# Recurrence products and negated maxima in PSUM, the heads' root on VectorE, y and bonus summed ahead of centring

## The reference, cut to what matters

```
# layer 1, for each sequence, head (8 x 8 state s) and token
a     = k[:, None] * v[None, :]
out   = einsum(r, faaaa * a + s)        # r . s ("y") plus r . (faaaa * a) ("bonus")
s_new = a + w[:, None] * s
y = (y - mean8(y)) * rsqrt(var8(y) + 1e-5) * gn_w + gn_b   # per head of 8 channels
# layer 2, self and cross attention
scores = scores * mask - 10000 * (1 - mask)
probs  = softmax(scores)                # exp(scores - max) / sum
# layer norms: (x - mean) / sqrt(var + 1e-5)
```

## Time and profile before

| | |
|---|---|
| median of 3 runs | 1115.88 us (1115.58 to 1124.76) |
| the profiled execution, its own time | 1123.09 us |
| its span | 1121.3 us |
| TensorE busy | 1006.8 us (90%) |
| VectorE busy | 817.9 us (73%) |
| GpSimd busy | 567.8 us (51%) |
| ScalarE busy | 555.1 us (50%) |
| mean granted TensorE clock | 0.957 |

### The profile page before, as it was taken

The page is one execution under the profiler, slowest core; times in us unless marked ns, Lnnn a source line. Parts: engine busy times, 40 slices in busy tenths (PEclk is TensorE's granted clock), DMA queues, the critical chain, the costliest instruction groups (busy, mean ns, idle before and its releaser), DMA issues.

```text
span 1121.3 us, 27159 instructions
## 1 busy us (share of the span) xinstructions
PE 1006.8 (90%) x10816; PEld 802.3 (72%) x10816; DVE 817.9 (73%) x1679; ACT 555.1 (50%) x1354; POOL 567.8 (51%) x634
## 2 busy tenths in 40 slices
PE   5868999998777889999999999999987978999997
PEld 3647877766556678888877877776665757878886
DVE  1233268879999888988546357569998999997675
ACT  2479573322223236546676875642222333756663
POOL 1354155557565565554344354456655655664331
PEclk9979999989979899999999999999996988999999
DMA  8501000000000000000101010010000000000001
GB/s 345 212 2 25 25 25 1 25 0 1 1 1 1 2 31 1 32 32 2 52 22 45 10 38 23 3 25 1 1 1 1 1 2 12 2 13 12 12 2 40
DMA packets 28172, 30.35 MB, mean 27 GB/s; under 512 B 16528, under 2 KB 24976, under 8 KB 27280
## 3 DMA queue, kind: packets, MB, share of 16 engines
q1 hardware_dynamic: 28048, 28.63, 7.7%
HBM read 26.52 MB, written 2.10 MB: 26 GB/s over the span
## 4 chain that ended last, share of the span: by engine, by line
PE 56%; DVE 21%; DVEq 10%; issue 5%; POOL 3%; ACT 2%; POOLq 2%; ACTq 1%; DMA 1%; SPq 0%
PE bank L489 7%; PE bank L501 7%; PE bank L363 6%; PE bank L375 6%; PE bank L396 6%; PE bank L388 4%; DVEq L1006 3%; DVEq L864 3%; PE bank L520 3%; DVE lane L1010 3%; DVE lane L865 2%; PE bank L452 2%; PE bank L529 2%; DVE lane L809 2%; PE bank L432 2%
## 5 line engine op out<-in xcount | busy, mean ns | idle before, releaser
L1365 POOL TENSOR_TENSOR lane<-lane 128x512 f32<-128x512 f32 x160 | 166.6, 1047 | 220.8 <-DVE lane L884 126.2
L1164 ACT COPY lane<-bank 128x512 f32<-128x512 f32 x240 | 135.9, 587 | 216.7 <-PE bank L363 82.6
L363 PE MATMUL bank<-ident,lane 128*128 128x128 f32 x896 | 135.1, 287 | 26.0 <-DVE lane L809 15.4
L363 PEld LDWEIGHTS bank<-ident,lane 128*128 128x128 f32 x896 | 106.6, 146 | 53.2 <-DVE lane L809 18.5
L1433 POOL TENSOR_TENSOR lane<-lane 128x512 f32<-128x512 f32 x64 | 83.6, 1311 | 87.1 <-DVE lane L1010 87.1
L1010 DVE TENSOR_TENSOR_SCAN lane<-lane 128x256 f32<-128x256 f32 x128 | 99.9, 821 | 5.8
L1228 ACT ACTIVATE lane<-bank,lane 128x128 f32<-128x128 f32 x256 | 91.0, 374 | 25.9 <-DVE lane L934 24.7
L1186 ACT ACTIVATE lane<-lane 128x512 f32<-128x512 f32 x96 | 60.6, 635 | 72.9 <-DVE lane L865 72.5
L1146 ACT ACTIVATE lane<-bank,vecs 128x256 f32<-128x256 f32 x112 | 55.8, 552 | 73.1 <-PE bank L363 72.6
L1351 POOL TENSOR_TENSOR lane<-lane,scalars 128x2 f32<-128x2 f32 x56 | 41.2, 736 | 73.5 <-DVE lane L801 70.6
L882 DVE TENSOR_REDUCE lane<-lane 128x8 f32<-128x512 f32 x96 | 64.7, 674 | 11.6 <-ACT lane L1186 11.3
(11 more groups left out here) (157 smaller groups left out, 2293.1 us busy)
## 6 DMA issues: line engine op xcount, KB each, us to landing
lane<-in_inT SPq DMA_DIRECT2D x16, 256.0 KB, 5.2
lane<-in_x SPq DMA_DIRECT2D x16, 256.0 KB, 2.8
w_d<-in_w_d SPq DMA_DIRECT2D x1, 3072.0 KB, 24.6
w_am<-in_w_am SPq DMA_DIRECT2D x1, 2048.0 KB, 11.3
lane<-in_inT SPq DMA_DIRECT2D x16, 128.0 KB, 3.0
lane<-in_ctx SPq DMA_DIRECT2D x8, 256.0 KB, 2.7
out_x<-lane SPq DMA_DIRECT2D x8, 256.0 KB, 2.2
w_c<-in_w_c SPq DMA_DIRECT2D x1, 1792.0 KB, 15.6
```

The lines of the kernel that those rows point to most:

```text
L363: ins = pe.transpose(t[:, i * P:(i + 1) * P], src, ident[:, :])
L1164: s.copy(out, src).then_inc(bk.free_sem(key), 1)
L1365: p.tensor_tensor(q, q, den.unsqueeze(2).to_broadcast([P, n, 512 // n]), ALU.mult).then_inc(sig["normal"].sem, 1)
```

## The change

- `steps`: the copy of s0 by VectorE is gone. TensorE writes s0 into the token-0 columns of the spread bank by one more matmul per state pair, with the identity as weights and 8 columns moving; the spread matmuls write tokens 1 to 63. The tile of k is widened by one column per sequence, holding 1.0, so that VectorE multiplies all 512 elements of the bank by k in place in PSUM. The scans read the products from PSUM and write the state to SBUF. The bank is freed after the scans, by a drain of its own.
- `shift` and `masked`: in self and cross attention the negated maxima are written into the score bank (its first 8 columns, whose scores were already taken) and read from there by the addition that follows; the bank is freed by that addition, no longer by the masking. The signal "shifted" goes, and GpSimd waits for a new signal "masked". Layer 3 keeps its tile.
- y and bonus: VectorE adds the bonus to y on the way from the bank to SBUF, in place of ScalarE's copy; the centring is two matmuls a group (of 256 columns each) in place of four.
- The root: the seed, the Newton steps (three instructions each) and the spreading over sequences move from GpSimd to VectorE, behind the addition of 1e-5.
- `v_variance`: its drain and addition of 1e-5 move to GpSimd, ahead of the power, with a drain there. Statistics and application stay on VectorE.
- The mixes are opened as (w, k) and (v, r, g). TensorE waits for the small per-group input once before the first spread. All order strings and BANKS are new.

The diff, its core:

```
             def spread_values(m, i0):
                 t = [pe_open(pe, (g, "spread", m, i)) for i in (i0, i0 + 1)]
                 for e in range(2):
                     for n in range(2):
                         q = slice(32 * (i0 + n), 32 * (i0 + n) + 32)
-                        ins = pe.matmul(t[n][:, e * T:(e + 1) * T], spread[q, e, :], L.bv[q, m, :], start=True, stop=True)
-                        if e == 1:
-                            ins.then_inc(bk.full_sem((g, "spread", m, i0 + n)), 1)
+                        pe.matmul(tokens(t[n][:, e * T:(e + 1) * T])[:, :, 1:S], spread[q, e, :], tokens(L.bv[q, m, :])[:, :, 0:S - 1],
+                                  start=True, stop=True)
+                for n in range(2):
+                    i = i0 + n
+                    pe.matmul(t[n][:, :].rearrange("p (e b t) -> p e b t", e=2, b=G)[:, :, :, 0], ident[:, :], L.s0[:, m, 2 * i:2 * i + 2, :],
+                              start=True, stop=True).then_inc(bk.full_sem((g, "spread", m, i)), 1)
...
-                pe.matmul(t[:, m * T:(m + 1) * T], centre, L.bonus[:, m, :], start=True, stop=False)
-                ins = pe.matmul(t[:, m * T:(m + 1) * T], centre, L.yc[:, m, :], start=False, stop=True)
+                ins = pe.matmul(t[:, m * T:(m + 1) * T], centre, L.yc[:, m, :], start=True, stop=True)
...
             for tt in range(TT):
-                v.bn_aggr(L.mv[:, tt, :], L.stats[:, tt, :])
-            v.drain()
-            v.tensor_scalar(L.mv[:, :, 1], L.mv[:, :, 1], 1e-5, None, ALU.add).then_inc(sig["variance"].sem, 1)
+                ins = v.bn_aggr(L.mv[:, tt, :], L.stats[:, tt, :])
+            ins.then_inc(sig["variance"].sem, 1)
...
-            def shift(j, src):
-                v.tensor_reduce(A.nmax[:, j, :], src, AX_X, ALU.max, negate=True)
+            def shift(j, src, nmax):
+                v.tensor_reduce(nmax, src, AX_X, ALU.max, negate=True)
                 v.drain()
-                return v.tensor_tensor(grid(A.probs[j]), src, A.nmax[:, j, :].unsqueeze(2).to_broadcast([P, n, S]), ALU.add)
+                v.tensor_tensor(grid(A.probs[j]), src, nmax.unsqueeze(2).to_broadcast([P, n, S]),
+                                ALU.add).then_inc(bk.free_sem((g, tag, "scores", j)), 1)
...
-                    shift(j, grid(A.probs[j])).then_inc(sig["shifted"].sem, 1)
+                    shift(j, grid(A.probs[j]), bk.tile((g, tag, "scores", j))[:, 0:n])
...
                 st = L.state[:, 2 * i:2 * i + 2, :, :]
-                v.tensor_copy(st[:, :, :, 0], L.s0[:, m, 2 * i:2 * i + 2, :])
-                src = bk.tile(key)[:, :].rearrange("p (e b t) -> p e b t", e=2, b=G)
-                kt = tokens(L.bk[:, m, :])
-                v.tensor_tensor(st[:, :, :, 1:S], src[:, :, :, 0:S - 1],
-                                kt[:, :, 0:S - 1].unsqueeze(1).to_broadcast([P, 2, G, S - 1]), ALU.mult).then_inc(bk.free_sem(key), 1)
+                kv = bk.tile(key)[:, :].rearrange("p (e b t) -> p e b t", e=2, b=G)
+                v.tensor_tensor(kv, kv, L.bk[:, m, :, 0:S].unsqueeze(1).to_broadcast([P, 2, G, S]), ALU.mult)
                 v.drain()
                 w = L.wS[:, m, :, :].rearrange("p b t -> p (b t)")
                 for e in range(2):
-                    s = st[:, e, :, :].rearrange("p b t -> p (b t)")
-                    ins = v.tensor_tensor_scan(s, w, s, 0.0, ALU.mult, ALU.add)
+                    ins = v.tensor_tensor_scan(st[:, e, :, :].rearrange("p b t -> p (b t)"), w, bk.tile(key)[:, e * T:(e + 1) * T], 0.0,
+                                               ALU.mult, ALU.add)
                 ins.then_inc(sig["scanned"].sem, 1)
+                v.drain().then_inc(bk.free_sem(key), 1)
...
+            key = (g, "y")
+            v.wait_ge(bk.full_sem(key), bk.full_at(key))
+            v.tensor_tensor(flat(L.yc[:, :, :]), bk.tile(key)[:, :], flat(L.bonus), ALU.add).then_inc(bk.free_sem(key), 1)
+            yield
...
+            v.tensor_scalar(var, bk.tile(key)[:, 0:S], 1e-5, None, ALU.add).then_inc(bk.free_sem(key), 1)
+            v.drain()
+            v.tensor_scalar(r.bitcast(I32), var.bitcast(I32), -0.5, RSQRT_SEED, ALU.mult, ALU.add)
+            v.drain()
+            for _ in range(3):
+                v.tensor_tensor(t, r, r, ALU.mult)
+                v.drain()
+                v.scalar_tensor_tensor(t, t, -0.5, var, ALU.mult, ALU.mult)
+                v.drain()
+                v.scalar_tensor_tensor(r, t, 1.5, r, ALU.add, ALU.mult)
+                v.drain()
+            v.tensor_tensor(tokens(L.rstd_rows), r.unsqueeze(1).to_broadcast([P, G, S]), own_batch.unsqueeze(2).to_broadcast([P, G, S]),
+                            ALU.mult).then_inc(sig["rstd_own"].sem, 1)
...
+            else:
+                p.tensor_scalar(L.mv[:, :, 1], L.mv[:, :, 1], 1e-5, None, ALU.add)
+            p.drain()
```

More of the change, by code:

```diff
@@ L83 @@
     "PE": (
[L84 to L87, removed]
@@ L633, in pe_b @@
                 if n == 0:
-                    mix(MIXES[2:4])
+                    mix(MIXES[2:5])
                     yield
@@ L689, in pe_b @@
             yield
-            pe.wait_ge(bk.free_sem((g, "bonus")), bk.taken_at((g, "bonus")))
             pe.wait_ge(bk.free_sem((g, "y")), bk.taken_at((g, "y")))
@@ L895, in v_attention @@
                         v.wait_ge(bk.full_sem((g, tag, "scores", PT_ - 1)), bk.full_at((g, tag, "scores", PT_ - 1)))
-                    shift(j, grid(bk.tile(key)[:, :])).then_inc(bk.free_sem(key), 1)
+                    shift(j, grid(bk.tile(key)[:, :]), A.nmax[:, j, :])
                     yield
@@ L967, in v_b @@
             v.memset(L.wS[:, :, :, 0], 0.0)
+            v.memset(L.bk[:, :, :, 0], 1.0)
             yield
@@ L1372, in p_attention @@
                 if step < PT_ and tag != "l3":
-                    key = (g, tag, "scores", step)
-                    p.wait_ge(bk.free_sem(key), bk.taken_at(key))
+                    p.wait_ge(sig["masked"].sem, sig["masked"].at(g, PART[tag] + step + 1))
                     if tag == "self":
@@ L1434, in p_b @@
                     yield
-            key = (g, "var_y")
-            p.wait_ge(bk.free_sem(key), bk.taken_at(key))
-            x, r, t = L.yw[:, 0, :], L.yw[:, 1, :], L.yw[:, 2, :]
-            p.tensor_scalar(r.bitcast(I32), x.bitcast(I32), -0.5, RSQRT_SEED, ALU.mult, ALU.add)
-            p.drain()
-            for step in range(3):
-                p.tensor_tensor(t, r, r, ALU.mult)
-                p.drain()
-                p.tensor_tensor(t, t, x, ALU.mult)
-                p.drain()
-                p.tensor_scalar(t, t, -0.5, 1.5, ALU.mult, ALU.add)
-                p.drain()
-                p.tensor_tensor(r, t, r, ALU.mult)
-                p.drain()
-            p.tensor_tensor(tokens(L.rstd_rows), r.unsqueeze(1).to_broadcast([P, G, S]), own_batch.unsqueeze(2).to_broadcast([P, G, S]),
-                            ALU.mult).then_inc(sig["rstd_own"].sem, 1)
-            yield
         def p_c(p, g):
```

99 lines of the change are left out of this document (48 added, 51 removed).

## The result

The changed kernel takes **1088.66 us** (median of 4 runs, 1087.44 to 1090.60) against 1116.34 us (4 runs, 1115.58 to 1124.76) of the kernel before on the same chip: a ratio of **0.9737, 95% interval 0.9687 to 0.9787**. That is 27.7 us, more than double the 13 that I forecast, though inside the range; it is 4 us from the time that I gave to the rival "latency comes back too".

What follows compares the result with a forecast made beforehand. VectorE was taken to bound two stretches, TensorE the rest. VectorE's terms sum to -14 us, TensorE's to +1, so -13 from an expected median of 1115.9 gives 1103 us; range 1083 to 1127.

Steps and rivals of the forecast that it cites:

- latency comes back too: Faster rival: shorter root and relieved GpSimd leave TensorE fewer gaps in the VectorE stretches, clock stays up; 1085 us, chance 0.20.
- scans: VectorE's scans reading PSUM: 635 ns each, 68 of them in the VectorE stretches, -10.0 us.
- Identity matmuls: TensorE's 128 added records of 8 columns at 0.12 us each, +15 us, half in stretches that TensorE sets.
- the prediction's own rule: A microsecond off VectorE counts about one in the VectorE stretches, nearly nothing outside; the reverse holds for TensorE.
- the mixes: On TensorE, mix g runs beside two mixes using other rows of the array, saving 8 us.
- the root's term: Root moved to VectorE: 4.4 us a group, six groups in the VectorE stretches, +26 us; its shorter chain gives little.
- VectorE stretches: The windows 224 to 504 and 784 to 1008 us, where VectorE is busy 91% and TensorE idles 69.7 us.
- The 1e-5 of the layer norms: Addition and drain moved from VectorE to GpSimd, 32 of 48 in the VectorE stretches, taken as -11 us.
- the maxima: Negated maxima in PSUM: 60 two-SBUF additions in the VectorE stretches fall to 692 ns, -19.6 us.
- Paid back elsewhere: No-change rival: stretches shift, savings fall where TensorE is full, or GpSimd holds up the root; 1115 us, chance 0.22.
- Banks held too long: Slower rival: score banks freed 5.7 us later, TensorE waits at 16 openings; 1127 to 1135 us, chance 0.15, shared.
- Product in the same bank: Slower rival: reading and writing one PSUM bank takes turns, doubling the product instruction; 1126 us, within a shared 0.15.

Runs made afterwards that it cites:

- e11: The changed kernel without the identity matmuls, spreads again 256 columns wide, s0 left out: 1082.60 us, ratio 0.9676.
- e3: The changed kernel with the root back on GpSimd, all else kept: 1131.68 us, ratio 1.0120.
- e17: The kernel before with all parts of the change but the root, best searched orders: 1144.81 us (3 runs; a fourth took 1798.41), ratio 1.0209.
- e14: The work of the changed kernel under the best orders and banks from a search: 1121.62 us, ratio 1.0022.
- e5: The kernel before, old orders, with the root alone moved to VectorE: 1140.78 us, ratio 1.0196.
- e18: The kernel before with the root alone on VectorE, best searched orders and banks: 1160.49 us, ratio 1.0378.
- e7: The kernel before, old orders, with the layer norms' 1e-5 alone moved to GpSimd: 1119.11 us, ratio 0.9998.
- e12: The changed kernel with the layer norms' drain and addition of 1e-5 back on VectorE: 1086.04 us, ratio 0.9720.
- e8: The changed kernel without the nine Newton instructions, the root left as the bare seed: 1078.56 us, ratio 0.9631.
- e9: The changed kernel with the negated maxima in SBUF again, the bank still held until the shift: 1103.37 us, ratio 0.9867.
- e4: The changed kernel with the products written to SBUF and scanned there in place: 1098.98 us, ratio 0.9815.
- e2: The kernel before, old orders, with products in PSUM, root on VectorE and layer norms' 1e-5 on GpSimd: 1139.72 us, ratio 1.0192.
- e10: The changed kernel with the maxima in SBUF and the score bank freed at the masking: 1104.26 us, ratio 0.9877.
- e6: The kernel before, old orders, with the products in PSUM alone, including identity matmul and own drain: 1124.71 us, ratio 1.0064.
- e1: The changed kernel's orders, banks, mixes and y plus bonus with old maxima, products, root and layer norms: 1172.98 us, ratio 1.0475.
- e13: The work of the kernel before under the best orders and banks from a search: 1150.35 us, ratio 1.0285.

## Why the prediction was wrong

**The sign, the range and most of the rows held; the size did not.** Taken one by one against "what the profile would show": L865 688 and 692 ns (forecast 690), scans 674 (under 700), products 695 (680, and not 1300), no copy of 8 elements, the root 3.6 us (4 to 5). Identity matmuls took 0.153 us a record (0.12), and VectorE's work fell by 48.6 us (about 30), partly because the gate's L1038 lost 9.4 us of hold-up that I had not counted (the orders' doing, below).

**Mis-sized terms explain a part.** The sum again, with the measured durations and the prediction's own rule: root 6 x (3.6 - 4.4) = -4.8; the gate, three quarters of 9.4, -7; scans at 674 in place of 635, 68 x 0.04 = +2.7; the identity matmuls with what they do to the spreads are 22.9 us of TensorE's time (e11) where I had 15, half of the excess, +4; the mixes saved 9.8 us where I had 8, half of that, -0.9. Together -6: the sum would have been -19, and 9 us are still missing. The -7 of the gate was nothing that the prediction saw.

**The step that failed** is the root's term: +26 us as "the one large cost", with its shorter chain at nothing, because "this moves waiting, and gives little by itself". The runs show the opposite sign: put back on GpSimd in the changed kernel, the root costs 43 us under the fixed orders (e3) and 21 under searched ones (e17 against e14, about what two searches differ by), where the term says 26 saved. Alone in the old kernel it was +22 (e5) and +10 (e18, less than two searches differ by). So its price hangs on the work and the orders around it, and a sum of separate terms can't hold it.

The premise under it did not hold either: "a microsecond taken from VectorE is worth about one in the VectorE stretches and nearly nothing outside". The 1e-5 of the layer norms was worth nothing under either orders (e7 14.8 us of work for 0, e12 7.2 for -2). The Newton steps were worth 0.55 (e8, 12 for 22), the maxima 0.6 (e9, 14.5 for 24.8) and the products 0.8 (e4, 9 for 10.8), where the rule, by the part of each in the stretches, has 0.75, 0.94 and 0.53. Counted over the whole kernel, the 48.6 us that VectorE lost at 0.57 a microsecond would give 27.7 as well. But that price fails for the layer norms, and for the root it has the wrong sign: in e3 VectorE has 22.6 us less to do and the time is 43 us longer. So that agreement counts as chance here. A busy share of 91% on VectorE beside 86% on TensorE was not one engine at its bound but two that wait for each other in turn, as e2's windows suggest.

**The rivals.** "Latency comes back too" had the right time, 1085, and the right place: TensorE's gaps in those stretches, 69.7 to 32.4 us, with the clock up. By the prediction's own working they hold 0.10 x 280 + 0.04 x 224 = 37 us at 1.2 GHz now and held 75, the half that this rival let return. I gave it 0.20, because I took VectorE's 85% and more there as a wall; it was 83% and no wall. "Paid back elsewhere" is what happens under the old orders, which the change does not keep. "Banks held too long" decides from 0.8 us an opening; e10 against e9 shows nothing (0.1%, inside both intervals), under orders made for the longer hold, and TensorE's one wait that a shift ends, L376 for L865, is of 2.9 us. "Product in the same bank" would have shown 1300 ns and showed 695.

**The two places where a page bears on it.** The scans from a bank took 660 ns at least and 675 in the median, those from SBUF 658 at least; L863 writing a bank 678 against 667. The Trainium skill (VectorE: DVE Perf Modes, section on the TRN2 errata) would have a PSUM source cost more, by an estimate from its table 65 ns; the traces do not agree, as the prediction held. L865 with two SBUF inputs took 691 to 1680 ns, 1044 in the median, and 686 to 690 with one input in PSUM. The Trainium skill (SBUF — State Buffer, section on its two separate sides) says that VectorE with two SBUF inputs and GpSimd reading SBUF exclude each other for a whole instruction; the spread of these durations agrees.

**What stays open.** How much of the 34 us of TensorE's waits each part removed, since an order shares them out anew; how much of e3's 43 us is misfit of its orders; what the maxima and the sum of y and bonus are worth alone; and whether e12's orders, fitted to it, would gain more.

## What to carry to other kernels

Where the order of instructions is written out, a part's price under the old order says little: the same root was +22 us alone and 43 us of gain as the last piece, so price a change together with a new order. Count the idle time of the busiest engine that its chains cause, and beside it what the clock takes behind such gaps: in e3 more than half of the loss was the same matmuls taking longer. Two engines at about 90% that both idle in the same stretch are a sign of turns taken, where shorter dependent chains count more than busy time. Rival times that rest on waits deserve as much chance as the sum of the busy terms.

## What the runs showed of the hardware

- Matmuls that use 32 rows of the array each ran side by side, and a matmul over all 128 rows between them ended that. Sixteen records of the spreads in a row took 1.16 us, and eight by themselves 1.13 with 256 columns and 1.12 with 252. With the identity matmuls between, the 256 records took 36.1 us; without, 23.9 (before) and 20.5 (e11). I had priced this at nothing. In the same way mix g, beside two others, cost nothing more: 27.96 us for all mixes became 18.17.
- By busy time a record, a matmul of 8 columns with 128 x 128 weights took as long as one of 128 columns: 0.153 us against 0.148 (132.4 us for 896).
- How long VectorE is held up changes with what runs beside it: L1038 with 256 elements took 1370 ns in the median before, and its successor 484 in the change. Its mean was 1168 before and in e7 (1164), 817 in e5 and 845 in e6 under the same orders, 619 in e1 and 642 in e13 with the old work under other orders. So neither the order nor the work decides it alone.
- Multiplying 512 elements in place in one PSUM bank takes 695 ns, 9 more than into SBUF (686 in e4).
